# GpSimd sums the five base rows of one chunk before TensorE turns them

## What is computed

```python
offsets = _conv2d(x, off_w, off_b)
aw = jax.nn.sigmoid(_conv2d(x, attn_w, attn_b))
gx = gx_base[None, None, None, None, :] + off[:, :, :, 0] * (2.0 / W)
gy = gy_base[None, None, None, :, None] + off[:, :, :, 1] * (2.0 / H)
...
sampled = corner(y0, x0, wy0 * wx0) + corner(y0, x1, wy0 * wx1) + corner(y1, x0, wy1 * wx0) + corner(y1, x1, wy1 * wx1)
head_out = jnp.einsum('nhckxy,nhkxy->nhcxy', sampled, awr)
combined = head_out.reshape(N, OUT, Ho, Wo_sp)
return jnp.einsum('oc,nchw->nohw', Wo, combined)
```

## Time and profile before

| | us |
|---|---|
| median of 3 runs | 130.2 |
| lowest and highest | 130.07, 130.41 |
| the profiled execution, its time | 129.84 |
| the profiled execution, its span | 128.0 |

### The profile page before, as it was taken

How to read it: one execution, slowest core, us unless ns; L and a number is a source line. 1 busy time by engine, 2 the same in 40 slices (tenths; PEclk the granted TensorE clock), 3 DMA queues, 4 the chain that set the end, 5 groups by cost and what they waited for, 6 DMA issues and landing times.

```text
span 128.0 us, 3078 instructions
## 1 busy us (share of the span) xinstructions
PE 112.8 (88%) x1226; PEld 95.2 (74%) x1226; DVE 100.0 (78%) x221; ACT 60.0 (47%) x120; POOL 46.6 (36%) x70
## 2 busy tenths in 40 slices
PE   3999979949999989999899989788779999899770
PEld 2788769939999879998799879666656766576550
DVE  5649999999999499950999899996561989976620
ACT  3989789727905678009693546110301441313100
POOL 8970000426700793049700199996040020222000
PEclk9999999999999999999999999999999999999999
DMA  2840000039989996300000000000000000000033
GB/s 79 236 94 0 0 0 0 8 103 256 234 200 230 234 207 135 70 5 0 0 0 0 5 0 3 0 0 5 3 0 5 5 5 0 0 5 0 18 72 82
DMA packets 9069, 7.35 MB, mean 57 GB/s; under 512 B 4796, under 2 KB 7934, under 8 KB 9054
## 3 DMA queue, kind: packets, MB, share of 16 engines
q1 hardware_dynamic: 8446, 6.62, 22.6%
q10 hardware_dynamic: 608, 0.52, 1.6%
HBM read 2.22 MB, written 0.52 MB: 21 GB/s over the span
## 4 chain that ended last, share of the span: by engine, by line
DVE 39%; PE 35%; issue 11%; POOL 4%; DMA 3%; SPq 3%; ACT 2%; POOLq 1%; DVEq 1%
DVE prod L889 12%; PE bank L1301 7%; PE bank L1208 6%; DVE part L897 5%; PE bank L1183 5%; DVE part L849 4%; PE bank L1321 4%; PE bank L1334 3%; DVE prod L933 3%; DMA w_v_s<-in_w_v 3%; PE bank L1160 3%; PE bank L1148 2%; DVE g_cross L857 2%; DVE w_cross L862 2%; PE bank L1194 2%
## 5 line engine op out<-in xcount | busy, mean ns | idle before, releaser
L897 DVE TENSOR_TENSOR part<-vd,bank 128x512 f32<-128x512 f32 (+2 forms) x25 | 19.5, 829 | 7.2 <-PE bank L1194 7.1
L889 DVE TENSOR_TENSOR prod<-hat,prod 128x576 f32<-128x576 f32 (+2 forms) x25 | 21.8, 936 | 0.0
L1208 PE MATMUL bank<-cst,part 128*128 128x128 f32 x168 | 20.0, 273 | 0.0
L1183 PE MATMUL bank<-cst,prod 128*128 128x128 f32 x144 | 17.5, 272 | 2.6 <-DVE prod L889 2.6
L1208 PEld LDWEIGHTS bank<-cst,part 128*128 128x128 f32 x168 | 18.6, 140 | 0.8 <-DVE part L897 0.4
L1183 PEld LDWEIGHTS bank<-cst,prod 128*128 128x128 f32 x144 | 16.0, 140 | 3.1 <-issue 2.0
L343 POOL TENSOR_TENSOR prod<-prod 128x640 f32<-128x640 f32 (+1 forms) x5 | 6.4, 1279 | 27.1 <-DVE prod L889 27.1
L1105 PE MATMUL bank<-ones_r 128*128 128x512 f32 x46 | 13.4, 446 | 3.0 <-POOL w_pair L430 2.1
L1160 PE MATMUL bank<-w_cross,g_cross 128*128 128x432 f32 (+1 forms) x90 | 15.5, 320 | 0.2 <-DVE w_cross L862 0.2
L1160 PEld LDWEIGHTS bank<-w_cross,g_cross 128*128 128x128 f32 x90 | 14.2, 189 | 0.8 <-issue 0.4
L438 POOL TENSOR_TENSOR ab<-ab,half_pow 128x2 f32<-128x2 f32 (+1 forms) x7 | 5.2, 745 | 25.2 <-DVE ab L725 25.1
(11 more groups left out here) (107 smaller groups left out, 190.7 us busy)
## 6 DMA issues: line engine op xcount, KB each, us to landing
vd<-vd SPq DMA_DIRECT2D x2, 600.0 KB, 7.6
vd<-vd SPq DMA_DIRECT2D x2, 560.0 KB, 10.5
vd<-vd SPq DMA_DIRECT2D x4, 224.0 KB, 4.6
vd<-vd SPq DMA_DIRECT2D x2, 300.0 KB, 4.0
prod<-in_w_off SPq DMA_DIRECT2D x1, 486.0 KB, 5.6
vd<-vd SPq DMA_DIRECT2D x2, 240.0 KB, 4.9
w_s<-in_w SPq DMA_DIRECT2D x4, 72.0 KB, 4.0
wc_s<-in_wc SPq DMA_DIRECT2D x2, 144.0 KB, 3.3
```

The source lines that it names most:

```text
L889: return nc.vector.tensor_tensor(cells[:, STEP0[i]:STEP0[i] + n], hat[:, c % 2, at + 3:at + 3 + n, 0:ck].rearrange("p d (k s) -> p d k s", ...
L897: return nc.vector.tensor_tensor(to.rearrange("p d (q e) -> p d q e", e=HD), moved_by, weights.unsqueeze(3).to_broadcast([P, n, cx, HD]), ...
L1183: last = nc.tensor.matmul(out_ps[0:size, b * P:(b + 1) * P], prod[:, at:at + size], ident, start=(b == 0 and t == 0), stop=(b == n - 1 and ...
L1208: last = nc.tensor.matmul(comb_bank[:, j * P:(j + 1) * P], part[:, n % PARTS, d, j * P:(j + 1) * P], ident, start=(m == 0 and d == 0 and j ...
```

## The change

For chunk 1 alone (`POOL_ADDS = 1`) GpSimd doesn't signal after each base row. It multiplies the five rows as before and then adds them up in place in three additions, each waiting for the one before by a new semaphore `base_parts`: rows 0 and 1 plus rows 2 and 3 (512 elements in each partition), then row 0 plus row 1, then row 0 plus row 4 (256 each). Only the last raises `base_ready`, once. TensorE waits for that one signal and transposes row 0 alone, 2 transposes where there were 10. `bases_made` counts one signal for this chunk. The three lines of additions are 477, 479 and 481 of the changed kernel; every line behind them is 15 higher than before (line 1208 becomes 1223), those of `apply_bases` 4 higher (line 462 becomes 466).

```diff
+POOL_ADDS = 1
...
         def bases_made(c, rows):
-            return 1 + (c - 1) * ND + rows if c else 1
+            if c <= POOL_ADDS:
+                return c + min(rows, 1) if c else 1
+            return 2 + (c - 2) * ND + rows
...
-                    nc.gpsimd.tensor_tensor(
+                    last = nc.gpsimd.tensor_tensor(
                         part[:, ND - 1, i, 0:w * C].rearrange("p (q e) -> p q e", e=HD),
                         v[:, i, x0:x0 + w, :].rearrange("p x (h e) -> p (x h) e", e=HD),
                         cell[:, i, 0:w * HEADS].unsqueeze(2).to_broadcast([P, w * HEADS, HD]),
-                        ALU.mult).then_inc(base_ready, 1)
+                        ALU.mult)
+                    if c != POOL_ADDS:
+                        last.then_inc(base_ready, 1)
+                if c == POOL_ADDS:
+                    last.then_inc(base_parts, 1)
+                    rows = part[:, ND - 1, :, 0:w * C]
+                    pool.wait_ge(base_parts, 1)
+                    nc.gpsimd.tensor_tensor(rows[:, 0:2], rows[:, 0:2], rows[:, 2:4], ALU.add).then_inc(base_parts, 1)
+                    pool.wait_ge(base_parts, 2)
+                    nc.gpsimd.tensor_tensor(rows[:, 0], rows[:, 0], rows[:, 1], ALU.add).then_inc(base_parts, 1)
+                    pool.wait_ge(base_parts, 3)
+                    nc.gpsimd.tensor_tensor(rows[:, 0], rows[:, 0], rows[:, 4], ALU.add).then_inc(base_ready, 1)
...
-                w, nd = CHUNKS[c][1], sum(STEPS_X[i][1] for i in APPLY[m]) or ND
+                w, nd = CHUNKS[c][1], sum(STEPS_X[i][1] for i in APPLY[m]) or (1 if c == POOL_ADDS else ND)
```

More of the change, by code:

```diff
@@ L240, in build @@
         base_ready = sem("base_ready")
+        base_parts = sem("base_parts")
         off_ps = sem("off_ps")
```

## The result

| | median us | lowest to highest | runs |
|---|---|---|---|
| kernel before | 130.13 | 129.77 to 130.51 | 14 |
| changed kernel | 131.0 | 130.57 to 132.09 | 14 |

The ratio is 1.0066 with a 95% interval of 1.0047 to 1.0086: the change makes the kernel 0.6 to 1.1 us slower. 130.9 was forecast, slower by 0.5%. The profiled execution of the changed kernel took 130.9 us with a span of 129.1, against 129.84 and 128.0.

What follows compares the result with a forecast made beforehand. TensorE's row-sum transposes of chunk 1 and the convolution behind them were taken as the bound; 0.88 us won and about 1.6 given back as TensorE's wait make +0.7, so 130.2 + 0.7 = 130.9 us, range 129.6 to 131.3.

Steps and rivals of the forecast that it cites:

- TensorE is the path at this place: Chunk 1's row-sum transposes and the convolution behind bound the kernel; 8 fewer transposes save 0.88 us.
- Alone, the additions would be in time: GpSimd's three additions, undisturbed, end at 51.95 us, over 1.1 us before TensorE needs them.
- Whole-instruction exclusion, in turn: GpSimd and VectorE, on SBUF operands, alternate by whole instructions near 49 us; about 1.6 us given back as TensorE's wait.
- VectorE first: At 49 us VectorE's line 933 starts 0.03 us ahead of GpSimd's first addition; forecast's chance 0.57.
- rival 1: GpSimd's first addition gets in ahead of VectorE's line 933 at 49 us: -0.5 us, 129.7 us; chance 0.26.
- VectorE's loss is covered: VectorE's delay in chunk 2's products, +2.2 us in sum, falls into its 4.58 us of idle time, costing nothing.
- The start from rest, +0.06: TensorE's restart after waiting for the third addition: load to matmul 0.17 us against a pitch of 0.11, adding 0.06.
- A handover that costs 0.25 more: Each GpSimd addition begins late and takes its whole time, ending 0.25 us later; sum about +1.4 us.

Runs made afterwards that it cites:

- e1: Changed kernel without GpSimd's three additions, TensorE turning row 0 alone, rows 1 to 4 left out of the output; ratio to the kernel before 0.9912.
- e3: Changed kernel with VectorE waiting ahead of chunk 2's first product until GpSimd's third addition is over; ratio to the kernel before 1.0029.
- e6: Changed kernel with VectorE waiting for GpSimd's multiplications ahead of chunk 2's first product, so the first addition goes first; ratio to the kernel before 1.0007.
- e2: Changed kernel with a VectorE memset of one element per partition ahead of chunk 2's first product; ratio to the kernel before 1.0065.
- e4: Changed kernel with the first addition alone, TensorE turning rows 0, 1 and 4 (6 transposes); ratio to the kernel before 0.9962.
- e5: Changed kernel with all three additions and TensorE turning all five base rows of chunk 1 again (10 transposes); ratio to the kernel before 1.0113.
- e7: Changed kernel with the first two additions, TensorE turning rows 0 and 4 (4 transposes); ratio to the kernel before 0.9954.
- e9: As e6, but the new wait replaces one VectorE had there, so the number of waits is as before; ratio to the kernel before 0.9990.
- e8: The changed kernel run again, unaltered, beside the others on the same chip; ratio to the kernel before 1.0074.
- e10: The kernel before with only a VectorE memset of one element per partition added ahead of chunk 2's first product; ratio to the kernel before 1.0024.

## Why the prediction was right, point by point

- **TensorE is the path at this place.** Right: e1 gets 0.87 us of the computed 0.88.
- **Alone, the additions would be in time.** Right: e3 has them at 1.29, 0.73 and 0.73 us, computed 1.28, 0.73 and 0.73. They would be 53.0 - 51.95 = 1.05 us ahead of TensorE, not over 1.1.
- **Whole-instruction exclusion, in turn.** Right. Computed 2.8, 0.8 and 1.7 us for the additions, measured 2.75, 0.82 and 1.72; line 938 (953) computed near 1.5, measured 1.52; the first of line 889 (904) near 1.9, measured 1.87; the end of the third addition computed 54.54, measured 55.06 - 0.56 = 54.50. The added 0.01 us of a VectorE instruction that waited fits two of its three rows; for 640 elements it is 0.02, which changes nothing in the sum. The rule of the Trainium skill, SBUF — State Buffer, section "Who interferes with whom", an exclusive lock taken by whichever issues first, is borne out by e3, e6 and the changed kernel together: 2.75 us or 1.28 for the same addition by 0.03 to 0.05 us of issue time. That it takes two SBUF operands on VectorE is read from the rows of before, where line 897 with PSUM leaves GpSimd alone; no experiment changes the operands.
- **VectorE first.** Right in both profiles of the changed kernel, each by 0.03 us. Four more kernels without a wait for it have the same order (e2, e4, e5, e7), with leads of 0.01 to 0.03 us, so it isn't left to chance from execution to execution. But the prediction couldn't know that: it had one reading of 0.03 us, of a kind that e2 shows to be no finer than that. That the tie fell its way was luck in part, as the 0.26 for the other side says; e6 shows that the other side of it was computed right too (-0.5 us forecast for rival 1, -0.56 at the place).
- **VectorE's loss is covered.** Right: idle 3.00 us in place of 4.58, computed 3.1; GpSimd's base sums of chunk 2 at 58.96 - 0.56 = 58.40, computed 58.4. e3 shows what it costs when the cover is used up.
- **The start from rest, +0.06.** Wrong, by about 0.1. The two weight loads after the wait take 0.20 us together, in place of a pitch of 0.11 and 0.14 for the last, so the second begins 0.06 after the first, and the first at 55.11 - 0.56 = 54.55, where 54.59 was computed; TensorE makes up 0.05 us in place of losing 0.06. This is why +0.59 stands at the place and not +0.7.
- **A handover that costs 0.25 more**, worked out from what the Trainium skill, SBUF — State Buffer, section "A bandwidth-pool intuition that's wrong (but worth ruling out)", measured for a DMA: not seen. No addition ends later than by the forecast's own terms.
- **The time.** The ratio gives +0.86 us, forecast +0.7, trace +0.57. A part of such gaps is the clock: at full clock e1, e4, e5, e7 and e9 lie within 0.11 us of their traces. The changed kernel is still above its own, in e8 by 0.14 us, and so are e2 and e6, by 0.18 and 0.20 after their longer stop of 0.23 is counted, all within the uncertainty. In the first comparison the clocks of the kernel before are not on record, so its 0.86 can't be divided that way. The start of the program moves by some tenths between executions, and the kernel against itself gives 0.2 us by the ratio and 0.1 at full clock. What is left of the gap stays open.

## What to carry to other kernels

When work is handed to GpSimd, look first at what VectorE reads at that time: beside instructions with two SBUF operands, a GpSimd instruction costs up to its own length plus the length of VectorE's (2.75 us for 1.28 and 1.65 here), and the order of issue decides which engine pays; 0.08 us of it moved TensorE by 1.15. Count the turns until the signal that another engine waits for, and stop handing over one turn before it comes late; here two additions gain and the third loses more than all three could win. A delay that is covered at one place (VectorE's products) can come back at the next, where the same pair meets without cover.

## What had not been expected of the hardware

One more entry in VectorE's program, a memset that costs nothing where it stands or one more wait, lengthens a stop of VectorE some 67 us later from 0.81 or 0.82 to 1.20 us of idle time, and moves what is behind it by 0.23 us (in e6 the last two convolution stretches start 3.79 us apart, in the kernel before 3.56). It is there in all four kernels with such an entry (e2, e3, e6, e10) and in none of the nine other profiles, e9's among them, which has e6's order without the entry. All four entries stand ahead of chunk 2's first product. No row shows the cause.

A memset of one element per partition ahead of a large instruction on VectorE doesn't delay it measurably: in e2 the product still leads GpSimd's addition by 0.03 us.
